# Ten of the thirty-six scatters of node sums moved from GpSimd to SyncE, as row transfers with addresses held in a register

## The chip, the core and the metric

One core of a Trainium2 chip runs the whole kernel. The metric is the device time of one execution in microseconds, as the median over the runs. One further execution is profiled; its rows are what the text below argues from, and its times are taken from the start of its span.

## What is computed

A graph has 6250 nodes with 16 features each and 200000 edges (a source node, a destination node, 16 edge features), sorted by destination. Two layers follow each other. Cut to what matters:

```
w_m = (edge @ W_msg  + b_msg ).reshape(E, 16, 16)
w_a = (edge @ W_attn + b_attn).reshape(E, 16, 16)
h   = x[src][:, :, None]
attn = softmax of (w_a * h) over the edges of one destination
x = layernorm(x + sum over edges and input features of (w_m * h * attn))
x = layernorm(x + mean over the edges of a destination of edge)
```

So each node needs two rows of 16 sums over its incoming edges: the attention sum and the mean of the edge features.

## The kernel before, in words

The nodes are ranked by their number of edges and dealt into NC = 49 tiles of 128 nodes, one node a partition, so that the nodes of a tile have about equally many edges. Tile k has DEG[k] edge slots (38 for tile 0, then 56 down to 22 in an order written out by hand), and a slot is one edge of each of the 128 nodes. The slots of a tile are cut into groups of 6 or 8, 221 groups in all. NODE[:, k] holds the node numbers of tile k.

For each slot **GpSimd** issues one indirect DMA that gathers the 128 source rows of x from DRAM (line 658, 1607 in all), and for each tile one that fetches its edge records (line 663). The gathered features go into a ring of FR = 80 slots. **TensorE** transposes the edge features (line 1105), makes the two weight matrices of each edge (line 1116), and sums over the slots with an identity (line 1136). **VectorE** multiplies weights by features (line 1486) and messages by exponentials (line 1499), takes the means of the edge features (line 1511, counted by the semaphore v_sa) and divides (lines 1518 to 1520). **ScalarE** evacuates, takes exponentials, and writes the attention sums of tile k into OUTR[:, k, 0:16] (line 905, counted by a_out).

The order on every engine is written out as a list of steps: in a step one group is produced and an earlier one consumed. Each engine runs its own list in order.

What happens to the sums around the change: the first MAIN = 36 tiles are written from OUTR to a table y_d in DRAM, one row of 32 float32 (128 B) for each node, at the address that the node number gives. This is done by the function results(k) on GpSimd (line 701): an indirect DMA, a scatter, with 128 rows. It stands in GpSimd's list behind the gathers of tile k + 5, so the first one comes after the gathers of tile 5 and the last one after those of tile 40. y_d has been filled with zeros at the start, by SyncE (line 489, semaphore d_yz). Each scatter adds 16 to d_y.

**SyncE** (SP), after the loads at the start, enters its function regular(). It waits until d_y counts all MAIN scatters (line 505), loads x and the table y_d back in plain node order (lines 506 and 507), waits for the layernorms, and writes the output (lines 510 to 512). On VectorE the layernorms of these nodes are fourteen pieces, main(0) to main(13), that are put one a step into the list from step NORMS on; main(0) waits for both loads and adds them (line 1559). These waits stand in the middle of VectorE's list: the work of the later tiles is behind them.

The last REST = 13 tiles never go through the table: GpSimd gathers x for them (line 709), does the layernorms of nine of them itself (lines 714 to 756), VectorE those of the last four (lines 1582 to 1602), and GpSimd scatters the finished rows to the output (line 759).

A register load from SBUF occurs once on each engine, in the function fork (line 434), with a compare and branch behind it (line 435).

Of the kernel before, what the change touches and what calls it, by code (L numbers as in the profile page):

```python
# [9 lines left out]
NP = 128 * NC  # L10
# [44 lines left out]
RK1 = NC - 1  # L55
MAIN = NC - 13
REST = NC - MAIN
BATCH = [(0, REST - 4), (REST - 4, REST)]
DEG = [c + c % 2 for c in CAPS]
THIRDS = [[(d * x // 3, d * (x + 1) // 3) for x in range(3)] for d in DEG]  # L60
# [38 lines left out]
for g in range(NGR):  # L99
    n = GRP[g][2]  # L100
# [9 lines left out]
STEPS, MADE, USED, p, c = [], {}, {}, 0, 0  # L110
# [17 lines left out]
for g in range(NGR):  # L128
    k, n = GRP[g][0], GRP[g][2]
# [30 lines left out]
def gnn_kernel(nc, xt, dst, src, ea, eat, es, wc, cst, cst2, out):  # L160
# [10 lines left out]
    YD = nc.dram_tensor("y_d", [NP, 32], f32, kind="Internal").ap()  # L171
# [3 lines left out]
    with ctx:  # L175
        def sb(name, shape, dt=f32):
            return ctx.enter_context(nc.sbuf_tensor(name, shape, dt))

        def sem(name):
            return ctx.enter_context(nc.semaphore(name))  # L180
# [185 lines left out]
        OUTR = reg([128, NC, 32])  # L366
# [3 lines left out]
        NODE = reg([128, NC], i32)  # L370
# [6 lines left out]
        STI = spare[:, 16 * NC:19 * NC].bitcast(i32).rearrange("p (x c) -> p x c", c=NC)  # L377
        STS = spare[:, 19 * NC:19 * NC + 3 * REST].rearrange("p (x c) -> p x c", c=REST)
        SSI = spare[:, 19 * NC:19 * NC + 3 * REST].bitcast(i32).rearrange("p (x c) -> p x c", c=REST)
        YS = CS[:, 128:128 + 16 * REST].rearrange("p (c w) -> p c w", w=16)  # L380
        SQS = YN[:, 0:REST, 0:16]
        YB = YN[:, :, 0:16]
# [3 lines left out]
        VIO = sb("VIO", [128, 1])  # L386
        RCL = sb("RCL", [128, REST])

# [19 lines left out]
        S = {n: sem(n) for n in names}  # L408
# [3 lines left out]
        d_bl = [sem(f"d_bl{i}") for i in range(8)]  # L412
        d_st = [sem(f"d_st{i}") for i in range(4)]
        d_dt = [sem(f"d_dt{i}") for i in range(2)]
        d_xe = [sem(f"d_xe{i}") for i in range(3)]
        d_ea = [sem(f"d_ea{i}") for i in range(2)]
        d_h0 = [sem(f"d_h0_{a}") for a in range(LAST[0] + 1)]
        d_hl = [sem(f"d_hl{a}") for a in range(LAST[NC - 1] - FIRST[NC - 1] + 1)]
# [54 lines left out]
        def _(sp):  # L473
# [28 lines left out]
                features(q)  # L502

            def regular():
                sp.wait_ge(S["d_y"], 16 * MAIN)
                sp.dma_start(XNN, xt[0:NP, :].rearrange("(p c) k -> p c k", c=NC)).then_inc(S["d_xn"], 16)
                sp.dma_start(YN[:, :, :], YD.rearrange("(p c) w -> p c w", c=NC)).then_inc(S["d_yl"], 16)
                sp.wait_ge(S["v_ln"], 1)
                for p0, p1 in ((0, 112), (112, 127)):
                    sp.dma_start(out[p0 * NC:p1 * NC, :].rearrange("(p c) k -> p c k", c=NC), XNN[p0:p1, :, :])\  # L510
                      .then_inc(S["d_out"], 16)
                sp.dma_start(out[127 * NC:N, :].unsqueeze(0), XNN[127:128, 0:N - 127 * NC, :]).then_inc(S["d_out"], 16)
                sp.wait_ge(S["d_out"], 48)
                sp.wait_ge(S["d_ou"], 16 * REST)
# [102 lines left out]


            fork(sp, regular, general)

        @block.gpsimd
        def _(g):
# [53 lines left out]
            def regular():  # L676
# [9 lines left out]
                def feats(k):  # L686
                    g.wait_ge(d_xe[k % 3], 16 * (k // 3 + 1))
                    for h in range(FIRST[k] + (k == 1), LAST[k] + 1):
                        if FOLD[h] is not None:
                            g.wait_ge(S["v_mult"], FROM[FOLD[h] + 1])  # L690
                        for m in range(k + 1, min(k + 3, NC)):
                            if EDGES[m] == h:
                                runs_of(m)
                        gather(k, h)
# [3 lines left out]
                def results(k):  # L698
                    g.wait_ge(S["a_out"], k + 1)
                    g.wait_ge(S["v_sa"], k + 1)  # L700
                    g.indirect_dma_start(YD, bass.IndirectOffsetOnAxis(ap=NODE[:, k:k + 1], axis=0), OUTR[:, k, :], None)\  # L701
                     .then_inc(S["d_y"], 16)

                for k in range(1, NC):
                    feats(k)
                    if 5 <= k < MAIN + 5:
                        results(k - 5)
                for k in range(MAIN, NC):
                    g.indirect_dma_start(YS[:, k - MAIN, :], None, xt, bass.IndirectOffsetOnAxis(ap=NODE[:, k:k + 1], axis=0))\  # L709
# [3 lines left out]
                def then(i):  # L713
                    done[0] += 1
                    i.then_inc(S["g_b"], 1)
                    g.wait_ge(S["g_b"], done[0])
# [29 lines left out]
                then(g.tensor_tensor(means, means, RCL[:, 0:REST - 4].unsqueeze(2).broadcast_to([128, REST - 4, 16]), ALU.mult))  # L746
                for b, (lo, hi) in enumerate(BATCH):
                    if hi < REST:
# [99 lines left out]


            fork(g, regular, general)  # L850

        @block.scalar
        def _(a):
# [35 lines left out]
            def regular():  # L889
# [13 lines left out]
                def result(k):  # L903
                    a.wait_ge(S["v_fin"], k + 1)
                    a.activation(OUTR[:, k, 0:16], FT2[:, k % 2, :], ACT.Copy, scale=POS[:, k:k + 1]).then_inc(S["a_out"], 1)
# [32 lines left out]
                for i in range(NST + 1):  # L938
# [22 lines left out]
                    if FINS.get(i - 4, NC) < NC - 2:  # L961
                        result(FINS[i - 4])
                lo, hi = BATCH[1]
                for x in range(2):
# [303 lines left out]
        def _(v):  # L1268
# [155 lines left out]
            def regular():  # L1424
# [169 lines left out]
                def last_batch():  # L1594
                    lo, hi = BATCH[1]
                    st = STS[:, :, lo:hi]
                    for x in range(2):
                        centre(lo, hi)
                        spread(SQS[:, lo:hi, :], st).then_inc(S["v_var"], 1)
                        v.wait_ge(S["a_z"], x + 1)  # L1600
                        link(v.reciprocal(STS[:, 0, lo:hi], STS[:, 2, lo:hi]))
                        i = v.tensor_tensor(YS[:, lo:hi, :], YS[:, lo:hi, :], wide(STS[:, 0, lo:hi]), ALU.mult)
                        if x == 0:
                            link(i)
                            added(lo, hi)
                    i.then_inc(S["v_ys"], 1)
# [399 lines left out]
```

## Time and profile before

| | |
|---|---|
| median of 3 runs | 2221.29 us (2220.6 to 2221.82) |
| the profiled execution's own time | 2220.79 us |
| its span, first to last instruction | 2218.9 us |
| granted TensorE clock, mean | 0.959 |
| busy: PE, DVE, ACT, POOL | 1965.3, 1819.1, 1252.1, 1662.2 us |

The time of the execution is 1.9 us more than its span. The engines' busy times overlap; SyncE is not in the list, since instructions that issue DMAs, load registers or wait are not counted as busy. They are shown with a q behind the engine's name (SPq), and a view of SP's own instructions gives their durations.

### The profile page before, as it was taken

What the parts mean: (1) busy time and instruction counts of PE and PEld (TensorE: products, weight loads), DVE (VectorE), ACT (ScalarE), POOL (GpSimd) and SP (SyncE); (2) the same over time, 40 slices, a digit from 0 to 9 for tenths busy, and PEclk for the clock granted to TensorE, in tenths of its full rate; (3) what the DMA queues carried; (4) which work ended last, traced back from release to release, by engine and by line L of the source; (5) the groups of instructions that cost most, each with busy time, mean ns of one, the idle gap of its engine ahead of it and who ended that gap; (6) DMA issues with size and microseconds to landing.
All of it is one profiled execution on the core that took longest, in us unless ns stands there. A gap on an engine that the chain in (4) does not pass through costs nothing.

```text
span 2218.9 us, 21991 instructions
## 1 busy us (share of the span) xinstructions
PE 1965.3 (89%) x6682; PEld 892.4 (40%) x6682; DVE 1819.1 (82%) x3094; ACT 1252.1 (56%) x1228; POOL 1662.2 (75%) x1791
## 2 busy tenths in 40 slices
PE   1697989978989899999999999998889998899995
PEld 0433434433444444444444444443434443344442
DVE  7787878876887888889888889878778888899984
ACT  4355646555555556566656566655555555466552
POOL 6777777777777777777777777777777777777776
PEclk9788999989999999999999999999999999999998
DMA  6201000000000001000000010000010000101000
GB/s 237 87 14 19 16 13 13 9 17 13 13 13 13 13 13 18 13 13 13 17 12 12 12 17 12 12 17 12 12 17 12 16 12 16 33 15 22 10 7 5
DMA packets 60074, 47.61 MB, mean 21 GB/s; under 512 B 28366, under 2 KB 55439, under 8 KB 59436
## 3 DMA queue, kind: packets, MB, share of 16 engines
q0 software_dynamic: 57632, 29.73, 8.5%
q1 hardware_dynamic: 2316, 16.40, 2.0%
q8 instruction: 56, 0.92, 0.2%
q14 instruction: 70, 0.57, 0.1%
HBM read 44.01 MB, written 1.90 MB: 21 GB/s over the span
## 4 chain that ended last, share of the span: by engine, by line
PE 44%; POOL 23%; DVE 18%; issue 11%; ACT 2%; DMA 1%; POOLq 0%; DVEq 0%; SPq 0%; ACTq 0%
PE PX L1136 33%; POOL AR L658 20%; PE PW L1116 8%; DVE AR L1486 8%; DVE AR L1499 3%; PE PTB L1105 2%; DVE AR L1518 2%; ACT PX L947 1%; POOL y_d L701 1%; DVE AR L1304 1%; POOL CS L709 1%; POOL out L759 1%; DVE AR L1520 0%; DVE AR L1511 0%; POOL AR L663 0%
## 5 line engine op out<-in xcount | busy, mean ns | idle before, releaser
L658 POOL DMA_INDIRECT AR<-in_xt,AR x1607 | 1526.2, 950 | 493.2 <-issue 478.8
L1136 PE MATMUL PX<-AR,CS 128*128 128x512 f32 x3246 | 1553.6, 603 | 7.3 <-ACT AR L901 6.2
L1486 DVE CUSTOM_DVE_ANT_1 AR<-PW,AR 128x1024 f32<-128x1024 f32 x815 | 970.5, 1220 | 256.4 <-PE PW L1116 99.3
L1136 PEld LDWEIGHTS PX<-AR,CS 128*128 128x128 f32 x3246 | 606.1, 193 | 522.5 <-issue 424.9
L1116 PE MATMUL PW<-WS,LT 100*128 100x512 bf16 x1630 | 511.7, 397 | 161.0 <-DVE AR L1486 157.7
L1499 DVE TENSOR_TENSOR AR<-AR,PX 128x1024 f32<-128x1024 f32 (+1 forms) x442 | 500.3, 1132 | 71.6 <-ACT PX L947 46.7
L953 ACT ACTIVATE PX<-AR 128x1024 f32<-128x1024 f32 (+1 forms) x221 | 212.4, 961 | 485.2 <-DVE AR L1499 483.7
L949 ACT ACTIVATE AR<-AR 128x2048 f32<-128x2048 f32 (+1 forms) x221 | 413.0, 1869 | 7.2
L1116 PEld LDWEIGHTS PW<-WS,LT 100*128 100x128 bf16 x1630 | 150.6, 99 | 654.1 <-issue 399.6
L947 ACT ACTIVATE PX<-AR 128x1024 f32<-128x1024 f32 (+1 forms) x221 | 231.5, 1047 | 119.0 <-DVE AR L1499 117.5
L895 ACT ACTIVATE LT<-PTB 100x1024 bf16<-100x1024 bf16 (+1 forms) x221 | 208.8, 945 | 127.3 <-PE PTB L1105 127.1
L1105 PEld LDWEIGHTS PTB<-IDB,AR 128*100 128x100 bf16 x1630 | 130.1, 132 | 64.1 <-issue 22.4
L1105 PE MATMUL PTB<-IDB,AR 128*100 128x128 bf16 x1630 | 135.6, 227 | 10.6 <-ACT AR L930 9.4
L901 ACT ACTIVATE AR<-PX 128x512 f32<-128x512 f32 x49 | 29.3, 597 | 155.5 <-PE PX L1136 155.5
L1518 DVE RECIPROCAL AR<-AR 128x256 f32<-128x256 f32 x49 | 85.5, 1746 | 2.7 <-ACT AR L901 2.7
L1486 DVE DVE_READ_ACCUMULATOR2_ANT AR<- 128x1 f32 x815 | 67.6, 83 | 0.0
L663 POOL DMA_INDIRECT AR<-in_es,E0I x48 | 45.8, 955 | 16.6 <-issue 12.8
L930 ACT ACTIVATE AR<-AR 128x1024 bf16<-128x1024 bf16 (+13 forms) x49 | 54.2, 1107 | 0.0
L922 ACT ACTIVATE AR<-AR 128x1024 bf16<-128x1024 bf16 (+13 forms) x49 | 54.1, 1103 | 0.0
L1511 DVE TENSOR_REDUCE AR<-AR 128x16 f32<-128x512 f32 (+13 forms) x49 | 52.6, 1073 | 0.0
L701 POOL DMA_INDIRECT y_d<-AR x36 | 36.2, 1006 | 11.0 <-issue 11.0
L1453 DVE TENSOR_TENSOR AR<-AR 128x160 f32<-128x160 f32 (+9 forms) x147 | 41.7, 340 | 0.1
(194 smaller groups left out, 451.9 us busy)
## 6 DMA issues: line engine op xcount, KB each, us to landing
AR<-in_xt,AR POOLq DMA_INDIRECT x1607, 2.3
AR<-in_eat SPq DMA_DIRECT2D x3, 3128.0 KB, 12.1
AR<-in_eat SPq DMA_DIRECT2D x1, 3120.0 KB, 12.1
y_d<-AR SPq DMA_DIRECT2D x1, 784.0 KB, 13.7
AR<-y_d SPq DMA_DIRECT2D x1, 784.0 KB, 4.7
AR<-in_es,E0I POOLq DMA_INDIRECT x48, 3.4
y_d<-AR POOLq DMA_INDIRECT x36, 2.1
CS<-in_cst SPq DMA_DIRECT2D x1, 455.0 KB, 5.4
```

Of the source, the lines that this page charges most:

```text
L658: g.indirect_dma_start(feat(h, j - j0, j - j0 + 1), None, xt, bass.IndirectOffsetOnAxis(ap=node, axis=0)).then_inc(hg_sem(h), 16)
L701: g.indirect_dma_start(YD, bass.IndirectOffsetOnAxis(ap=NODE[:, k:k + 1], axis=0), OUTR[:, k, :], None)\
L895: a.activation(LT[:, g % 3, 0:128 * n], PTB[0:K, 0:128 * n], ACT.Copy).then_inc(S["a_T"], 1)
L947: a.activation(half(w), x[:, 0:w, :], ACT.Exp, bias=shift).then_inc(S["a_x"], 1)
L949: a.activation(x, x, ACT.Exp, bias=shift).then_inc(S["a_exp"], 1)
L953: a.activation(half(w), x[:, w:2 * w, :], ACT.Copy).then_inc(S["a_x"], 1)
L1105: i = pe.transpose(PTB[0:K, 128 * j:128 * j + 128], part(k, 0, K)[:, j0 + j, :], IDB[:, :])
L1116: i = pe.matmul(PAIRS[s % 2][:, j, :], LT[:, g % 3, lo:lo + 128], WS[:, :], start=True, stop=True)
L1136: i = pe.matmul(PDR, IDN, x, start=(a == 0 and j == 0), stop=(g == LAST[k] and j == n - 1))
L1486: v.tensor_tensor_reduce(em(g, j, j + 2).rearrange("p (x c) -> p x c", c=32), w, hb, 1.0, LOW, ALU.mult, ALU.max, accum_out=MXC[:, k % 2, ...
L1499: v.tensor_tensor(y, y, EXP[:, 0:16 * w].rearrange("p (x o) -> p x o", o=16), ALU.mult).then_inc(S["v_gm"], 1)
L1518: link(v.reciprocal(RRT, d[:, 0:256]))
```

## The change

The function regular() of SyncE gets a loop ahead of its first wait. It waits until ten tiles' means and attention sums are written (v_sa and a_out at 10) and the table is zeroed. Then, for each of the 128 partitions and each of the first BYROW = 10 tiles, it loads the node number from NODE into a register and issues one DMA of one row of 32 floats from OUTR to y_d at that row. That is 1280 register loads and 1280 DMAs, whose landings are counted by four semaphores in turn. It waits for all of them, and then for the scatters that are left (d_y at 16 x 26). GpSimd's results() is called for tiles 10 to 35 only; its loop over one pair (0, 128) is the same single scatter as before.

```diff
@@ -55,6 +55,7 @@
 MAIN = NC - 13
 REST = NC - MAIN
+BYROW = 10
 BATCH = [(0, REST - 4), (REST - 4, REST)]
@@ -413,6 +414,7 @@
         d_xe = [sem(f"d_xe{i}") for i in range(3)]
+        d_rw = d_bl[0:4]
         d_ea = [sem(f"d_ea{i}") for i in range(2)]
@@ -502,7 +504,16 @@
             def regular():
-                sp.wait_ge(S["d_y"], 16 * MAIN)
+                sp.wait_ge(S["v_sa"], BYROW)
+                sp.wait_ge(S["a_out"], BYROW)
+                sp.wait_ge(S["d_yz"], 16)
+                for p in range(128):
+                    for k in range(BYROW):
+                        n = sp.value_load(NODE[p:p + 1, k:k + 1], min_val=0, max_val=NP - 1)
+                        sp.dma_start(YD[bass.DynSlice(n, 1), :], OUTR[p:p + 1, k, :]).then_inc(d_rw[p % 4], 16)
+                for x in range(4):
+                    sp.wait_ge(d_rw[x], 16 * 32 * BYROW)
+                sp.wait_ge(S["d_y"], 16 * (MAIN - BYROW))
                 sp.dma_start(XNN, xt[0:NP, :].rearrange("(p c) k -> p c k", c=NC)).then_inc(S["d_xn"], 16)
                 sp.dma_start(YN[:, :, :], YD.rearrange("(p c) w -> p c w", c=NC)).then_inc(S["d_yl"], 16)
                 sp.wait_ge(S["v_ln"], 1)
@@ -698,12 +709,13 @@
                 def results(k):
                     g.wait_ge(S["a_out"], k + 1)
                     g.wait_ge(S["v_sa"], k + 1)
-                    g.indirect_dma_start(YD, bass.IndirectOffsetOnAxis(ap=NODE[:, k:k + 1], axis=0), OUTR[:, k, :], None)\
-                     .then_inc(S["d_y"], 16)
+                    for lo, hi in [(0, 128)]:
+                        g.indirect_dma_start(YD, bass.IndirectOffsetOnAxis(ap=NODE[lo:hi, k:k + 1], axis=0), OUTR[lo:hi, k, :], None)\
+                         .then_inc(S["d_y"], 16)
 
                 for k in range(1, NC):
                     feats(k)
-                    if 5 <= k < MAIN + 5:
+                    if BYROW + 5 <= k < MAIN + 5:
                         results(k - 5)
```

## Rows read from the trace of the kernel before

**Rows 1.** The page: busy time of each engine, and the chain's shares

```profile
PE 1965.3 (89%) x6682; PEld 892.4 (40%) x6682; DVE 1819.1 (82%) x3094; ACT 1252.1 (56%) x1228; POOL 1662.2 (75%) x1791
...
PE 44%; POOL 23%; DVE 18%; issue 11%; ACT 2%; DMA 1%; POOLq 0%; DVEq 0%; SPq 0%; ACTq 0%
```

**Rows 2.** Waits of POOL, whole span: total us, times, longest us

```profile
POOL AR L658 <- issue: 478.8, 1571, 0.3
...
POOL y_d L701 <- issue: 11.0, 36, 0.3
POOL AR L658 <- DVE AR L1486: 8.2, 27, 0.3
```

**Rows 3.** Waits of DVE, 1400 to 1893 us: the longest

```profile
DVE AR L1486 <- DMA AR<-in_xt,AR: 88.0, 38, 4.0
```

**Rows 4.** The chain that ended last, 1880 to 2219 us: start us, us, what

```profile
1891.27 0.94 POOL AR L658
1892.52 2.15 DMA y_d<-AR
1895.06 4.69 DMA AR<-y_d
1899.87 0.99 DVE AR L1559
...
2066.36 1.05 POOL AR L663
...
2208.38 0.96 POOL out L759
```

**Rows 5.** Waits of SP, whole span: the two that bear on the change

```profile
SPq L506 <- DMA y_d<-AR: 1812.4, 1, 1812.4
...
SPq L510 <- DVE AR L1549: 119.7, 1, 119.7
```

**Rows 6.** Line 701, the scatters: duration ns min/median/max, first and last start us; landing

```profile
L701 POOL DMA_INDIRECT y_d<-AR x36: 1001/1001/1167, 347.5 to 1892.5; - x36
...
DMA to landing us min/median/max: 2.1/2.1/3.8
```

**Rows 7.** Line 701 in the stretch of the first ten: us, POOL busy, clock, DMA

```profile
340.00:815.00 475.00, 10.02 (x10) 0.97 0.09 13
```

**Rows 8.** Timeline of ACT: the tenth attention sum (line 905)

```profile
705.79 0.30 ACT L905 ACTIVATE AR<-AR 128x16 f32<-128x16 f32 x1
```

**Rows 9.** Line 905 in two stretches: us, ACT busy with (count), clock, DMA

```profile
0.00:700.00 700.00, 2.67 (x9) 0.94 0.15 38
700.00:710.00 10.00, 0.30 (x1) 1.00 0.08 8
```

**Rows 10.** Line 434, the only register load of SP: duration ns

```profile
L434 SPq TENSOR_LOAD <-TOT x1: 471/471/471, 81.7 to 81.7; - x1
```

**Rows 11.** Line 435, SP's compare and branch: duration ns

```profile
L435 SPq COMPARE_BRANCH  x2: 38/44/49, 82.3 to 2210.5; - x2
```

**Rows 12.** Timeline of SP: start us, us from first to last of those merged

```profile
4.36 0.26 SPq L478 DMA_DIRECT2D AR<-in_xt  x1
...
38.78 4.10 SPq L496 DMA_DIRECT2D WS<-AR  x6
...
1894.69 0.33 SPq L506 DMA_DIRECT2D AR<-in_xt  x1
1895.06 0.43 SPq L507 DMA_DIRECT2D AR<-y_d  x1
2015.19 0.87 SPq L510 DMA_DIRECT2D out<-AR  x2
2016.11 0.36 SPq L512 DMA_DIRECT2D out<-AR  x1
```

**Rows 13.** Waits of DVE, 1893 to 2219 us: those on gathers

```profile
DVE AR L1472 <- DMA AR<-in_xt,AR: 8.1, 4, 2.8
```

**Rows 14.** Timeline of the end: VectorE's last instruction, and POOL's tenth output scatter

```profile
2201.04 0.22 DVE L1602 TENSOR_TENSOR CS<-CS,AR 128x64 f32<-128x64 f32 x1
...
2204.60 0.95 POOL L759 DMA_INDIRECT out<-CS,AR  x1 [0.30 <-issue]
```

**Rows 15.** Stretches at the wait: PE, PEld, DVE, ACT, POOL busy, PE clock, DMA

```profile
1900.00:1910.00 10.00, 6.96 (x13) 3.11 (x14) 8.78 (x15) 5.05 (x5) 7.77 (x8) 0.60 0.07 8
```

**Rows 16.** The page: DMA queues, with packets, MB and share of 16 engines

```profile
q0 software_dynamic: 57632, 29.73, 8.5%
q1 hardware_dynamic: 2316, 16.40, 2.0%
```

## The prediction

> **What bounds the kernel now.** I read the page first: PE is the busiest engine and leads the chain, and POOL, at 75%, comes second in it [rows 1]. A 75% engine looks as if it had room, so next I read the waits of POOL. It has none: ahead of nearly every gather there is a fixed 0.3 us called issue, and even where a VectorE instruction is named as releaser the longest gap is 0.3 us [rows 2]. POOL issues without a pause, some 0.94 + 0.30 us a gather, and each scatter takes its turn in that stream. Whether POOL sets the end is told by who waits for its gathers. VectorE waits for them 38 times, 88.0 us in all, between 1400 and 1893 us [rows 3], so in that stage the gather stream is the bound. In the chain the stretch ends with the last scatter at 1892.52, the read of y_d at 1895.06, and VectorE's addition on line 1559 at 1899.87; VectorE and PE lead until 2066, and POOL from there to the last output scatter at 2208.38 [rows 4]. Finally SP: it waits 1812.4 us in one piece for the scatters [rows 5], which is why it can look free.
>
> **What is removed.** Ten scatters leave POOL between 340 and 815 us: 10.02 us busy [rows 7], 1.001 us each [rows 6], and 0.30 us of issue before each [rows 2], 13.0 us together. POOL is not held up by its ring (no gap over 0.3 us), so all later gathers move 13.0 us ahead. Until about 1400 this only lengthens their lead. Where VectorE waits for gathers it arrives 13.0 us sooner (88.0 us of waits are there to lose them from), and so does the tail, which POOL leads too. If nothing else happened the execution would take 2220.8 - 13.0 = 2207.8 us. The profiled execution, 2220.79 us, lies 0.5 us under the median; sums are made against it. The loop over one pair and the shared semaphores cost nothing: they change no executed instruction.
>
> **What is added.** 1280 register loads and 1280 DMAs in SP's order, ahead of the loads of x and y_d, on which VectorE waits in the middle of its list. They can start when ten attention sums are written. Nine are there by 700 us [rows 9], and the tenth ends at 705.79 + 0.30 = 706.1 [rows 8]; the means come earlier, and the earlier POOL doesn't move this, since no gather is waited for in that stage. The table must be complete at 1894.69 to cost nothing [rows 12]. Taking 2.1 us for the last landing, from the scatters [rows 6], 1186 us are left for 1280 rows: the point of decision is 0.927 us a row, and 0.917 us to keep the whole gain, since everything then comes 13.0 us sooner.
>
> A row's price, step by step. The load: 0.471 us, its only row [rows 10], and about 0.05 us to the next instruction, as between SP's last two lines (2015.19 + 0.87 to 2016.11) [rows 12]. The issue of the DMA: three output writes in succession, the last of them a single partition, take from 2015.19 to 2016.47, 0.427 us each with the gap [rows 12]; I take this, since they too go from SBUF to DRAM. The register arithmetic that turns a node number into an address and checks its bounds is not in the trace. I estimate two instructions of the length of SP's compare and branch, 0.044 us [rows 11], and 0.05 us of gap each: 0.188 us. Sum 0.471 + 0.05 + 0.427 + 0.188 = 1.136 us. All of it is serial: the address needs the register, and the next load stands behind the DMA.
>
> Bounds. From below, the shortest issue of all, 0.26 us [rows 12], no arithmetic and no gaps: 0.73 us, rows complete by 1643, nothing late. From above, the six transfers at 38.78, 4.10 us for six, 0.683 us each [rows 12], which were issued beside a large load: 0.471 + 0.05 + 0.683 + 0.188 = 1.392 us. I stay nearer the lower of these two issue prices because DMA is 9% busy in the stage [rows 7]. The bytes are no cost: 1280 rows of 128 B against the 16.40 MB that the queue carries now [rows 16].
>
> **What is late next.** At 1.136 us the last row is issued at 706.1 + 1454.1 = 2160.2 and lands by 2162.3. The wait that SP has today for the scatters becomes one for its own rows. Queued behind it on SP are the loads of x and y_d and then the output writes; VectorE stands at line 1559, with the multiplications of the later tiles behind it, and PE and ScalarE run dry. POOL runs on to the end of its ring and stops: its 13 us vanish in the stall. From SP's release to line 1559 it takes 1899.87 - 1894.69 = 5.2 us [rows 4, 12], and from there to the end of the span 2218.9 - 1899.87 = 319.0 us. Of this some comes back, because POOL has a full ring: the 8.1 us that VectorE still waits for gathers [rows 13], and 3.3 us at the end, where POOL reaches the last four tiles' scatters 3.3 us after VectorE is done (2204.60 against 2201.04 + 0.22) [rows 14]. Against this PE restarts slowly, as after today's 5.7 us of waiting, where its granted clock is 0.60 of the full 2.4 GHz over 10 us, so 1.2 GHz for most of them [rows 15]; I take back 8 us of the 11.4. With the 1.9 us outside the span: 2162.3 + 5.2 + 319.0 - 8.0 + 1.9 = 2480 us. In general the time is 1026 us plus 1280 times the price of a row, so each 0.1 us a row is 128 us.
>
> **A figure that speaks the other way.** The load's row says 0.471 us [rows 10]. The Trainium skill (Runtime: NRT & Kernel Launch, Instruction fetch mechanics) puts a register load at about 200 ns a register. By that a row would take 0.865 us, the table would be complete by 1815 us, and the change would gain: 2208 us. The same skill (DMA: Bandwidth & Descriptors, Latency and other measured facts) gives tensor_load a floor of about 600 ns, by which a row would take 1.265 us and the execution 2645 us. The trace's single load lies between the two and decides here; the first figure would lead to the first rival below.
>
> **The rivals.**
> - *SP keeps ahead.* If a row takes less than 0.917 us, the rows hide under the gathers and only the 13.0 us stay: 2207.8 us. For it: the load and the single-partition write of 0.36 us [rows 10, 12] make 0.83 us, and a load in a long sequence might be shorter than a lone one. Against it: gaps and arithmetic must then come to under 0.09 us. Chance 0.20.
> - *The issues are slow.* If back-to-back issues cost 0.683 us as at 38.78 us, the row is 1.392 us: 1026 + 1782 = 2808 us. For it: six issues in succession were that slow [rows 12]. Against it: a large load was under way there. Chance 0.14, with all above 1.32 us.
> - *One transfer at a time.* If a row had to land before the next started, 2.1 us each [rows 6] would make 1026 + 2688 = 3714 us. The gathers, issued every 1.25 us, overlap their landings, which speaks against it. Chance 0.02.
> - *The gain is not one.* If rows hide but the freed POOL time is swallowed at a full ring, 2221 us. With no gap over 0.3 us [rows 2] I give it, and rows that come just in time, 0.03.
>
> **How the numbers follow.** The forecast, a row between 0.96 and 1.32 us, has 0.61; its own range is 2255 to 2716 us. The range of 8 in 10 takes in the first rival and the forecast: 2207 to 2716. About 0.2% (4.4 us) is what a measurement can tell here. Faster by more: 0.20; within: 0.03; slower: 0.77.
>
> **What would show it.** SP's timeline after: a load and a DMA in alternation from 706 us on, the pitch of a row, and the last issue near 2160 us. VectorE's wait before line 1559 would grow from 5.7 to some 285 us, and POOL would show its first long gap, ending with VectorE's instructions; the scatters of line 701 would count 26. A pitch under 0.93 us, with line 1559 at about 1887 us, would prove the forecast wrong in its sign; a line 1559 far later than the rows' end would mean that the landings, not the issues, set the pace.

## The result, and the profile after

The changed kernel takes 2641.27 us (median of 4 runs, 2639.92 to 2642.74) against 2220.94 us: a ratio of 1.1893, with a 95% interval of 1.1876 to 1.1911. It is 420 us slower. The forecast was 2480 us, slower by 259 us: the sign and the mechanism were right, and one term, the price of a row, was too small.

The page of the changed kernel: its span, the busy times, three of the lines with the span in 40 slices of 66 us, and the chain's shares.

```profile
span 2640.9 us, 29656 instructions
...
PE 1963.9 (74%) x6682; PEld 891.5 (34%) x6682; DVE 1819.1 (69%) x3094; ACT 1252.4 (47%) x1228; POOL 1648.8 (62%) x1781
...
PE   2689899889989999999999989998400000059996
...
DVE  7777788678788889888888887888400000069995
...
POOL 6777777777777777777777777777750000026673
...
SPq 48%; PE 20%; issue 16%; DVE 14%; ACT 1%; DMA 1%; DVEq 0%; POOL 0%; POOLq 0%; ACTq 0%
```

The busy times of PE, DVE and ACT are those of before [rows 1] to within 2 us; POOL has 13.4 us less, of which the ten scatters are 10.0 us [rows 7]. No engine has more work, and yet the span is 422 us longer. The slices show where: behind the 29th PE and VectorE have six empty ones, and GpSimd five. And SP's sequencer, which had 0% of the chain before, now leads it with 48%.

SP's instructions for the rows, by line (512 is the register load, 513 the DMA): count, duration in ns as min/median/max, first and last start in us.

```profile
L512 SPq TENSOR_LOAD <-AR x1280: 278/487/652, 706.5 to 2326.0; - x183
L512 SPq FUSED_REGOPS  x1280: 152/152/186, 706.8 to 2326.5; - x183
L512 SPq SEQ_ASSERT  x1280: 18/18/37, 707.1 to 2326.7; - x183
```

```profile
L513 SPq FUSED_REGOPS  x1280: 37/37/48, 707.2 to 2326.8; - x183
L513 SPq MOVE y_d<-AR x1280: 37/38/45, 707.3 to 2326.9; - x183
L513 SPq DMA_DIRECT2D y_d<-AR x1280: 263/264/333, 707.3 to 2326.9; - x183
```

A row is six instructions. 1280 of them stand from 706.5 to 2326.0 us, so the pitch is (2326.0 - 706.5) / 1279 = 1.266 us. The six medians add up to 0.996 us; the other 0.27 us are the gaps between them, 0.045 us each on average.

The waits that answer to [rows 2, 3, 4] (total us, times, longest us), whole span. First three of VectorE before, then those after:

```profile
DVE AR L1486 <- PE PW L1116: 99.3, 95, 4.5
...
DVE AR L1499 <- ACT PX L947: 46.7, 33, 4.1
...
DVE AR L1559 <- DMA AR<-y_d: 5.7, 1, 5.7
```

```profile
DVE AR L1571 <- DMA AR<-y_d: 450.7, 1, 450.7
...
POOL AR L669 <- DVE AR L1498: 381.4, 19, 376.0
...
DVE AR L1498 <- PE PW L1128: 105.9, 103, 4.5
DVE AR L1498 <- DMA AR<-in_xt,AR: 65.0, 30, 4.0
...
DVE AR L1511 <- ACT PX L959: 52.1, 36, 4.1
...
POOL out L771 <- DVE CS L1614: 27.2, 1, 27.2
```

Lines 1571, 1498, 1511, 669 and 771 are lines 1559, 1486, 1499, 658 and 759 of before. VectorE waits 450.7 us for the table, where it waited 5.7. GpSimd, whose gathers never waited over 0.3 us for their ring, now waits 376.0 us in one piece for VectorE to free slots, and 27.2 us at the end for VectorE's last four tiles. VectorE comes to the table at 2333.28 - 450.7 = 1882.6 us, where it came at 1899.87 - 5.7 = 1894.2: 11.6 us sooner, and this gain is lost in the long wait. Its waits for gathers fell by more, from 88.0 to 65.0 us, but those for TensorE and ScalarE grew by 6.6 and 5.4 us.

The chain at the end of the rows, and the three stretches around the wait (us, PE, PEld, DVE, ACT, POOL busy, granted PE clock, DMA share, GB/s):

```profile
2325.98 0.49 SPq L512
2326.92 1.05 DMA y_d<-AR
2328.55 4.61 DMA AR<-y_d
2333.28 0.99 DVE AR L1571
```

```profile
700.00:1880.00 1180.00, 1112.13 (x3781) 504.62 (x3780) 1000.59 (x1666) 702.96 (x688) 893.62 (x941) 0.98 0.10 14
1883.00:2333.00 450.00, 0.00 (x0) 0.00 (x0) 0.00 (x0) 0.00 (x0) 58.74 (x63) 0.50 0.03 5
2333.00:2343.00 10.00, 6.55 (x10) 2.78 (x11) 8.90 (x15) 4.84 (x5) 4.81 (x6) 0.54 0.04 5
```

The addition that began at 1899.87 [rows 4] begins at 2333.28. In the 450 us before it PE, DVE and ACT do nothing at all, and GpSimd issues 63 more instructions, 61 gathers and 2 fetches of edge records, and stops. SP's last row lands 1.05 us after its issue. From the addition to the end of the span it takes 2640.9 - 2333.28 = 307.6 us, against 319.0 before.

### The profile page after: what moved, and what is told of

It reads as the page before. It is cut to its first block, busy times and chain, and to the rows that moved or that the text cites. A ratio compares the mean times of both kernels' runs of the same rounds, so it can differ in the third digit from the quotient of the medians.

```text
span 2640.9 us, 29656 instructions
## 1 busy us (share of the span) xinstructions
PE 1963.9 (74%) x6682; PEld 891.5 (34%) x6682; DVE 1819.1 (69%) x3094; ACT 1252.4 (47%) x1228; POOL 1648.8 (62%) x1781
## 4 chain that ended last, share of the span: by engine, by line
SPq 48%; PE 20%; issue 16%; DVE 14%; ACT 1%; DMA 1%; DVEq 0%; POOL 0%; POOLq 0%; ACTq 0%
SPq L512 32%; SPq L513 16%; PE PX L1148 15%; DVE AR L1498 5%; PE PW L1128 4%; DVE AR L1511 2%; DVE AR L1530 1%; PE PTB L1117 1%; DVE AR L1316 0%; ACT PX L959 0%; DVE AR L1523 0%; DVE AR L1532 0%; DVE AR L1531 0%; DVE AR L1465 0%; DVE AR L1474 0%
## 5 line engine op out<-in xcount | busy, mean ns | idle before, releaser
L1571 DVE TENSOR_TENSOR AR<-AR 128x784 f32<-128x784 f32 x1 | 1.0, 976 | 450.7 <-DMA AR<-y_d 450.7
```

## The experiments

Line numbers shift by one or two between these kernels; the table's addition on VectorE is line 1571 to 1574 in those whose lines are shown. Each diff shows only the lines that matter.

**The same rows, started earlier.** The loops are exchanged, and SP waits for one tile at a time:

```diff
-                sp.wait_ge(S["v_sa"], BYROW)
-                sp.wait_ge(S["a_out"], BYROW)
-                for p in range(128):
-                    for k in range(BYROW):
+                for k in range(BYROW):
+                    sp.wait_ge(S["v_sa"], k + 1)
+                    sp.wait_ge(S["a_out"], k + 1)
+                    for p in range(128):
```

> The same 1280 rows in another order: tile by tile, each tile's rows as soon as its own sums are written, instead of all ten after the tenth. Theory (SP's instructions of a row, 1.266 us in the changed kernel, run one behind the other from the moment they may start, and only their end counts): SP starts when the first sum is written, near 194 us, and is never held up by a later tile (162 us of rows a tile, tiles 43 to 99 us apart), so the last row is issued near 194 + 1621 = 1815 us, before the table is needed near 1882 us. Nothing stalls, and the ten scatters saved on GpSimd show: 2208 us, 13 us under the kernel before. Rival (1280 small writes disturb the gathers and the other engines wherever they stand, or GpSimd's saved time is swallowed): 2221 us or more although the rows end early.

Measured: 2208.65 us, ratio 0.9945 (0.9928 to 0.9962). Faster than before by 0.55%, with the same 1280 rows. SP's loads and two of its waits:

```profile
L512 SPq TENSOR_LOAD <-AR x1280: 281/487/683, 193.7 to 1813.9; - x183
```

```profile
SPq L510 <- ACT AR L917: 111.1, 1, 111.1
SPq L516 <- DMA y_d<-AR: 67.0, 1, 67.0
```

The load costs the same 487 ns and the rows take the same 1620 us, from 193.7 to 1813.9. But they end in time, and then SP waits 67.0 us for the scatters, the other way round from the changed kernel. 1280 small writes disturb nothing that shows in the time: the next run, without any, takes as long.

**The removed part alone.** The whole loop over rows is left out, with the waits ahead of it and behind it; nobody writes the first ten tiles' sums:

```diff
-                for p in range(128):
-                    for k in range(BYROW):
-                        n = sp.value_load(...)
-                        sp.dma_start(YD[bass.DynSlice(n, 1), :], ...).then_inc(d_rw[p % 4], 16)
```

> Leaves out the sums of the first ten tiles altogether: neither GpSimd nor SyncE writes them, so only the removed part of the change is left. Theory: GpSimd's stream is 10 x 1.30 us shorter and sets the pace from about 1400 us on, 2207.8 us. Rival (a full ring or another engine swallows it): 2221 us. If the run of rows tile by tile stands above this one, the difference is what 1280 small writes cost beside their own issue.

Measured: 2208.79 us, ratio 0.9945 (0.9928 to 0.9961). Ten scatters are worth 12 us, and the run before this one gets all of it.

**The added part alone.** GpSimd keeps its 36 scatters, and SP writes its rows to another table:

```diff
-                        sp.dma_start(YD[bass.DynSlice(n, 1), :], OUTR[p:p + 1, k, :])...
+                        sp.dma_start(YE[bass.DynSlice(n, 1), :], OUTR[p:p + 1, k, :])...
-                sp.wait_ge(S["d_y"], 16 * (MAIN - BYROW))
+                sp.wait_ge(S["d_y"], 16 * MAIN)
-                    if BYROW + 5 <= k < MAIN + 5:
+                    if 5 <= k < MAIN + 5:
```

> GpSimd keeps all 36 scatters, and SyncE's 1280 rows are written besides, to a table of their own that nobody reads, so only the added part of the change is left; the wait for them stays. Theory: VectorE waits for the end of SyncE's rows, and when GpSimd comes there is immaterial, so the ten scatters cost nothing here: 2641 us as in the changed kernel, within 3 us. Rival (the removed scatters still count): 2654 us.

Measured: 2641.07 us in one run. Where VectorE's arrival at the table is followed by a wait of hundreds of us, the ten scatters more or less are worth nothing: its wait is

```profile
DVE AR L1572 <- DMA AR<-y_d: 437.9, 1, 437.9
```

12.8 us less than in the changed kernel: VectorE arrives later by about the price of the ten scatters (13.0 us forecast), and the end is the same.

**Ten numbers at one load.** One load fills ten registers, and no check is made at run time:

```diff
+                regs = [sp.alloc_register(f"row{x}") for x in range(BYROW)]
                 for p in range(128):
+                    sp.reg_load(regs, NODE[p:p + 1, 0:BYROW])
                     for k in range(BYROW):
-                        n = sp.value_load(NODE[p:p + 1, k:k + 1], min_val=0, max_val=NP - 1)
+                        n = sp.snap(regs[k], min_val=0, max_val=NP - 1)
```

> The order and the start of the changed kernel, but one register load fetches the ten node numbers of a partition, and the bounds are stated without a check at run time. Theory (a row costs the sum of SP's instructions): of the 1.266 us the load (0.487 + 0.045) falls to a tenth, and the check (0.018) and most of the 0.152 us of fused register operations go: 0.5 to 0.75 us a row, last row at 706 + 640 to 960 = 1350 to 1670 us, so 2208 us. Rival (the pitch is set by the DMAs, one behind the other, and the load only waits for them): the pitch stays near 1.2 us, and the time near 2600 us.

Measured: 2208.83 us, ratio 0.9943 (0.9926 to 0.9959). Its loads, and its row transfers:

```profile
L512 SPq TENSOR_LOAD <-AR x128: 2094/2392/2510, 705.7 to 1556.1; - x128
```

```profile
L515 SPq MOVE y_d<-AR x1280: 29/29/42, 708.0 to 1562.4; - x183
L515 SPq DMA_DIRECT2D y_d<-AR x1280: 223/224/326, 708.1 to 1562.5; - x183
```

(1562.5 - 708.1) / 1279 = 0.668 us a row. The start at 706 us is unchanged and the pitch alone makes the rows end in time. A register still costs 2.392 / 10 = 0.239 us. The Trainium skill (Runtime: NRT & Kernel Launch, Instruction fetch mechanics) gives about 200 ns a register for loads in bulk; this load takes a fifth more, and those of four registers, in the last section, take 0.14 or 0.29 us a register.

**The DMA by itself.** The rows go to fixed places of a table that nobody reads:

```diff
-                        n = sp.value_load(NODE[p:p + 1, k:k + 1], min_val=0, max_val=NP - 1)
-                        sp.dma_start(YD[bass.DynSlice(n, 1), :], OUTR[p:p + 1, k, :])...
+                        n = BYROW * p + k
+                        sp.dma_start(YE[n:n + 1, :], OUTR[p:p + 1, k, :])...
```

> The 1280 row transfers of the changed kernel from the same sums, but to addresses fixed in the program, in a table nobody reads; no register loads. It leaves out the sums of the first ten tiles. Measures the price of the DMA by itself. Theory (each transfer costs SP its issue only): 0.25 to 0.35 us from one to the next, the last near 1110 us, time 2208 us. Rival (issues in succession cost what six of them cost in the kernel before, or one transfer waits for another): 0.6 us or more from one to the next; by either the table is ready in time, so the pitch in the trace decides, not the time.

Measured: 2206.69 us in one run. Its transfers:

```profile
L514 SPq DMA_DIRECT2D ye_d<-AR x1280: 214/252/453, 704.1 to 1086.4; - x183
```

(1086.4 - 704.1) / 1279 = 0.299 us from one to the next. So neither landings nor issues in succession hold SP up, and the six slow issues at 38.78 us [rows 12] are no price for these.

**The load by itself.** The loop keeps its value_load and loses its dma_start, and the waits for the landings go too:

```diff
-                        n = sp.value_load(NODE[p:p + 1, k:k + 1], min_val=0, max_val=NP - 1)
-                        sp.dma_start(YD[bass.DynSlice(n, 1), :], OUTR[p:p + 1, k, :])...
+                        sp.value_load(NODE[p:p + 1, k:k + 1], min_val=0, max_val=NP - 1)
```

> The 1280 register loads of the changed kernel with their checks, and no transfer; it leaves out the sums of the first ten tiles. Measures the load by itself. The first load of the loop took 0.278 us in the changed kernel, those behind a DMA 0.487. Theory (the load waits 0.2 us for the DMA issued just before it): without DMAs every load takes some 0.28 us, and the pitch is near 0.28 + 0.152 + 0.018 + three gaps = 0.6 us; last load near 1470 us, time 2208 us. Rival (loads in succession take 0.47 to 0.49 us by themselves): pitch near 0.8 us. By either the time is 2208 us, so the trace decides.

Measured: 2208.42 us in one run. Its loads, and the register operations behind them:

```profile
L512 SPq TENSOR_LOAD <-AR x1280: 260/273/431, 705.7 to 1421.1; - x183
L512 SPq FUSED_REGOPS  x1280: 147/147/186, 706.0 to 1421.4; - x183
```

The load takes 0.273 us where no DMA stands in front of it, and 0.487 us in the changed kernel, where one does. The pitch is (1421.1 - 705.7) / 1279 = 0.559 us. With the DMA's 0.299 us that makes 0.858 us; the row takes 1.266 us. Half of the difference, 0.214 us, is the longer load; most of the rest is the two instructions that only a computed address needs, 0.037 and 0.038 us, with their gaps. A row with a load and a DMA is dearer than a load and a DMA measured apart.

**Eight tiles, just too late.** The changed kernel with `BYROW = 8`:

```diff
-BYROW = 10
+BYROW = 8
```

> The changed kernel with eight tiles instead of ten, waiting for the eighth before the first row. Theory (each us by which the rows end late is a us of the execution): the eighth sum is written at 612.4 us, 1024 rows of 1.266 us end at 1908.8, 2 us later they have landed, 16 us after the scatters of the kernel before. That is 2220.8 + 16 = 2237 us, less up to 11 us that come back from GpSimd's fuller ring: 2226 to 2237 us, slower than before. Rival (a late table costs nothing until it is very late, since other work fills the wait): 2210 us, the gain of eight scatters.

Measured: 2225.31 us, ratio 1.0022 (1.0012 to 1.0031), just under the lower end of what the theory gave and far from the rival. Its chain at the table:

```profile
1908.11 1.04 DMA y_d<-AR
1909.73 4.81 DMA AR<-y_d
1914.66 0.99 DVE AR L1571
```

The addition comes 1914.66 - 1899.87 = 14.8 us later than before, the end of the span (2222.4) only 3.5 us later. The tail, from the addition to the end of the span, is 307.7 us, as in the changed kernel: 11.3 us come back already after this short wait. GpSimd is ahead in it, and at its end waits for VectorE's last tiles:

```profile
POOL out L771 <- DVE CS L1614: 15.2, 1, 15.2
```

Worked out from these numbers, and not run: a table that comes some 11 us late costs nothing against the kernel before, and from there on each us counts.

**Seventeen tiles, late and in time.** To use the two findings, rows are written in batches, each with one load a partition, as soon as its last tile is summed. The first version:

```diff
+                for lo, hi in [(0, 1), (1, 5), (5, 9), (9, 13), (13, 17)]:
+                    sp.wait_ge(S["v_sa"], hi)
+                    sp.wait_ge(S["a_out"], hi)
+                    for p in range(128):
+                        sp.reg_load(regs[0:hi - lo], NODE[p:p + 1, lo:hi])
+                        for k in range(lo, hi):
+                            n = sp.snap(regs[k - lo], min_val=0, max_val=NP - 1)
```

> A version meant to beat both: SyncE writes the rows of 17 tiles, first tile 0, then four tiles at a time as soon as the last of the four is summed, with one load for the four node numbers of a partition and no check of bounds at run time. From the run with ten at a load: 0.415 us a row and 0.24 us a register, so about 0.70 us a row, 355 us for four tiles. The start of the second batch is near 430 us, the end near 430 + 4 x 357 = 1860 us, just before the table is needed (1894.7 - 22.1 - 2 = 1870 us). Theory (GpSimd's stream sets the pace and is 17 x 1.30 us shorter): 2220.8 - 22.1 = 2198.7 us. Rival (beyond ten tiles something else takes over, TensorE or VectorE): 2205 us or more with no wait at the table. If the rows end late, each us shows.

Measured: 2243.62 us, ratio 1.0098 (1.0081 to 1.0115): a miss. My price of a row was 0.70 us. The 2048 rows of the last four batches stand from 431.1 to 1928.0 us, 0.731 us each, and so end 68 us after the 1860 us that I had worked out:

```profile
1928.05 1.30 DMA y_d<-AR
...
1929.94 4.81 DMA AR<-y_d
1934.87 0.99 DVE AR L1574
```

The tail of 2242.4 - 1934.87 = 307.5 us is the third of about this length. The same loop with batches (0, 2), (2, 6), (6, 10), (10, 14), (14, 16):

> The version with seventeen tiles, cut so that its rows end in time by what that run showed: SyncE writes the rows of 16 tiles, first tiles 0 and 1, then four at a time, then two. Four tiles took 374 us there; two take about 0.8 us a row, 205 us. So: 269 to 475, to 849, to 1224, to 1598, to 1803 us, ahead of 1872 us, when the table is needed. Theory (nothing stalls, GpSimd's stream is 16 x 1.30 us shorter): 2200.0 us. Rival (from somewhere beyond ten tiles GpSimd's stream no longer sets the pace, and another engine keeps the time): between 2201 and 2208 us with no wait at the table beyond some 6 us.

Measured: 2199.34 us, ratio 0.9904 (0.9887 to 0.992), 21 us under the kernel before, as the theory said. And with (0, 2), (2, 6), (6, 10), (10, 17):

> Seventeen tiles again, in batches of two, four, four and seven, so that the rows end near 1850 us, ahead of 1870 us, where the earlier run of seventeen ended at 1929 us. The work of GpSimd and the number of rows are those of that run; only the moment at which the rows end is moved. Theory (the end of the rows decides): 2198.7 us, 45 us under the earlier run of seventeen. Rival (2176 small writes cost that run its 23 us by load on the DMA engines, not by their end): 2225 us or more.

Measured: 2197.37 us, ratio 0.9894 (0.9878 to 0.9911), the fastest of all, 46 us under the other run of seventeen tiles with the same rows and the same scatters left to GpSimd. Its rows ended at 1610 us, not 1850, and SP and VectorE then waited as long as this:

```profile
SPq L519 <- DMA y_d<-AR: 263.2, 1, 263.2
```

```profile
DVE AR L1574 <- DMA AR<-y_d: 5.7, 1, 5.7
```

The theory holds from both sides: what a row on SP costs the execution depends on whether the rows end before the table is needed, and not on how many there are. The gain then goes by the scatters taken from GpSimd: 12, 21 and 23 us for 10, 16 and 17 of them.

## Why the prediction was right, and which term was mis-sized

- **What bounds the kernel, and what the removed part is worth.** Right. 13.0 us were forecast for ten scatters, and 12 us show in the run with nothing in their place and in both runs with ten tiles' rows that end in time. GpSimd's stream sets the pace up to the table.
- **When SP may start, and when the table is needed.** Right: the rows start at 706.5 us against 706.1, and VectorE comes to the table 11.6 us sooner than before, against 13.0.
- **The price of a row.** This is the step that was off: 1.136 us forecast, 1.266 us measured. 0.130 x 1280 = 166 us, less the 3.4 us by which the tail was shorter than forecast, is the 163 us between 2480 and the profiled execution's 2642.7 us. Inside the sum errors of both signs met. The DMA was put at 0.427 us with its gap, after output writes of up to 112 partitions; it takes 0.264 + 0.045 = 0.309 us. The register arithmetic was put at two short instructions, 0.188 us; it is four, 0.152 + 0.018 + 0.037 + 0.038 = 0.245 us with 0.18 us of gaps, more than twice as much. The load was put at 0.471 + 0.05 us and takes 0.487 + 0.045; that its one row [rows 10] came so near was luck, for by itself it takes 0.273 us, and only behind a DMA 0.487. The other working in the prediction, with a load of about 600 ns, came by luck to 1.265 us a row and 2645 us, nearest of all: the load is shorter than that, and the DMA and the arithmetic in it are the mis-sized ones.
- **What is late next.** Right in each part: the wait of VectorE (285 us forecast, 450.7 us with the dearer row), GpSimd running on for 63 instructions and stopping, its saved time gone; the run with the added part alone shows the last by itself.
- **The tail.** 311.0 us were forecast from the addition on, 307.6 measured. The 8.1 and 3.3 us that GpSimd's full ring gives back come back whole, 11.4 us: all of VectorE's 65.0 us of waits for gathers lie before the table, and at the end GpSimd waits for VectorE. The 3.4 us that I set against them for PE's slow restart should not have been there: the kernel before restarts too, with a granted clock of 0.60 over 10 us [rows 15] against 0.54 now, so its tail of 319.0 us already held such a restart.
- **The rivals.** SP keeps ahead: the point of decision, 0.927 us a row, was the right question, and at 0.668 us a row the rival comes true within 1.1 us. Slow issues and one transfer at a time: excluded by 0.299 us from one DMA to the next, and by 0.264 us for a DMA in the changed kernel itself. The gain is not one: excluded by the run without the rows, 12 us under the kernel before.

## What to carry to other kernels

An engine that waits most of the time is not free: it has a deadline. Before work is moved to it, divide the time between the moment the work may start and the moment someone waits for it by the number of pieces, and compare that with the sum of all instructions of one piece, gaps and address arithmetic included, measured in the order in which they will stand: here the parts by themselves add up to 0.858 us, and together they take 1.266. If it doesn't fit, ask first whether the work can start earlier; here the same rows, begun tile by tile, turned 420 us of loss into 12 us of gain, and with one load for several numbers, which made room for seven tiles more, it became 23.

## What the runs showed that I had not expected

A register load on SP costs 0.273 us by itself, and 0.487 us when a DMA was issued just before it. What it waits for, the trace doesn't say.

A load of four registers doesn't always cost the same. From the columns 2 to 5, 6 to 9 and 10 to 13 of a row of NODE (counted from 0) it takes 0.56 us, from the columns 1 to 4 and so on 1.15 us. The first line is the run with sixteen tiles in its second batch, the second the late run with seventeen, and the third the last batch of the run with sixteen, two registers from the columns 14 and 15:

```profile
L513 SPq TENSOR_LOAD <-AR x98: 501/562/752, 475.9 to 699.9; - x98
```

```profile
L513 SPq TENSOR_LOAD <-AR x127: 1047/1152/1348, 431.1 to 799.4; - x127
```

```profile
L513 SPq TENSOR_LOAD <-AR x128: 664/745/907, 1380.7 to 1593.1; - x128
```

This is the main reason why the rows of the runs with sixteen tiles and with seventeen in time ended at 1596 and 1610 us, over 200 us earlier than I had worked out. That the start of the four columns decides, their alignment, fits the loads of four; no run moves the start alone. It can't be all: two registers from column 14, four columns on from 10, take 0.745 us, more than four do from 10. The cause stays open.
